# Four edits to a gated two-layer block: weight remainders moved ahead of the units, a guard row as one fp32 product, two products on GpSimd, a norm on ScalarE

## The chip, the cores and the metric

The kernel runs on one core of a Trainium2 chip. The metric is the device time of one execution in microseconds (us). Names of engines: PE is TensorE, DVE is VectorE, ACT is ScalarE, POOL is GpSimd.

## The reference, cut to what matters

```python
x = x + tanh(g_xattn[0]) * wkv(w, u, layernorm(x), ctx)            # a decaying scan over 64 steps
x = x + tanh(g_ffn[0])   * ffn(layernorm(x), w_gate_up, w_proj)    # ternary weights, silu(gate)*up, rms norm, projection
x = x + tanh(g_xattn[1]) * attend(layernorm(x), ctx, mask)
x = x + tanh(g_ffn[1])   * linear(fp8(layernorm(x)), weight) + bias
# ternary_quant, on groups of 64 weights of a row:
#   scale = clip(mean(|w_g|), 1e-8);  q = clip(round(w_g / scale), -1, 1);  w_hat = q * scale
```

x has 16 x 64 tokens of 256 channels, w_gate_up is 2048 x 256 and w_proj 256 x 1024.

## The kernel before

The 1024 tokens lie in eight tiles of 128 and two halves of four tiles (h = 0 and 1). Every engine has its program written out by hand, and semaphores join them.

**Front.** For each half, PE turns the normed x to channel-major in banks 0 and 1 (`front_keys`, L712) and adds a guard, the product of a row that depends on the decay with the row of time steps 0 to 63. The row is split into three bf16 parts that DVE makes (L1382 to L1392) and that one bf16 product of 65 rows adds (L715). ACT exponentiates the result (`front_keys`, L511), and DVE multiplies it with the context (`wkv_product`, L1137), scans and divides it. Between these, PE transposes six blocks of 1024 weight columns (`weight_transposes`, L737) and ACT takes them to SBUF as `wT` (L529). PE keeps busy with six spare products (`keep_warm`, L971), sums absolute weights by group (`weight_sums`, L747) and brings half 0 back to token-major (`y_back`, L794).

**Remainders.** For each of the six blocks in QUANT_ORDER, `weight_rest(n)` makes scale minus absolute weight in a pair of PSUM banks: four products, two with a stationary operand of 24 rows (L765) and two of 128 (L767). ACT copies the pair to `wscale` (`rest_in(n)`, L535), and DVE quantizes the block in four instructions (`quant_here` and `quant_sign`, L1249, L1250, L1256, L1239). Only the pair 6, 7 is used, so that a remainder waits for the copy of the one before. Remainders 0 and 1 stand ahead of the first units, 2 just ahead of unit 0, 3 in unit 0, 4 in unit 1, 5 in unit 3.

**Units.** Sixteen units n of 128 tokens by 512 hidden columns. PE does `gate(n)` and `up(n)` (four products of 512 columns each, L845 and L846), turns unit n-1 back (`h_back`, L878), projects unit n-2 (L904) and subtracts the rounded part (`h_left`, L884). ACT does `silu(n)` (L576), then the square and the two parts of h of unit n-1 (L583, L587, L591). DVE multiplies gate and up to `hbuf` (`ffn_mul(n)`, L1284) and fits all other work between these. `linear_weight` (PE L945 and ACT L596) prepares the last layer's weight in unit 4. Half 1 of the first layer lies within units 3 to 6: DVE does both products (L1137), two scans, two residuals with statistics (`mix_pair`, `ln_stats`) and two norms (`ln_apply(1, 4, 2, 2)` and `(1, 6, 2, 3)`, L1127), whose reciprocal deviation POOL makes (`power`, L414 and L415). PE turns these tiles with `ffn_in(2)` ahead of gate 8 and `ffn_in(3)` ahead of gate 10 (L810).

Of the kernel before, what the change touches and what calls it, by code (L numbers as in the profile page):

```python
# [36 lines left out]
def gated_blocks(nc, x, ctx_in, mask, g_xattn, g_ffn, w_decay, u_bonus, w_gate_up, w_proj,  # L37
# [24 lines left out]
    QUANT_ORDER = [0, 1, 4, 2, 3, 5]  # L62
    SCALE_ROWS = 24
# [4 lines left out]
    GUARD_ROWS = 65  # L68
# [4 lines left out]
    with ExitStack() as ctx:  # L73
# [31 lines left out]
        t_row = sb("t_row", [GUARD_ROWS, CT], BF16)  # L105
        ngrow = sb("ngrow", [1, C])
        ngres = sb("ngres", [1, C])
        ngres2 = sb("ngres2", [1, C], BF16)
        ngparts = sb("ngparts", [GUARD_ROWS, C], BF16)
# [260 lines left out]
        def _(pool):  # L370
            own = [0]

            def link(ins):
# [18 lines left out]
            pool.memset(group_spread[:, :, :], 0.0).then_inc(spread_0, 1)  # L392
            pool.wait_ge(spread_0, 1)
            spread = group_spread.rearrange("m k (s c) -> m k s c", s=2)
            pool.affine_select(out=spread, in_=spread, compare_op=ALU.not_equal, fill=1.0, base=0,
                               pattern=[[-2, BLOCKS], [-1, 2], [0, 64]], channel_multiplier=1).then_inc(spread_ready, 1)
# [20 lines left out]

            power(0, 0, TPC, 1)
            power(0, TPC, TPC, 2)
            power_and_shift(1, 0, TPC, 1)  # L420
# [28 lines left out]
            power(1, 4, 2, 2)  # L449
            power(1, 6, 2, 3)  # L450
# [29 lines left out]
        def _(act):  # L480
# [50 lines left out]
            def rest_in(n):  # L531

                p = QUANT_ORDER[n]
                act.wait_ge(rest_ps, n + 1)
                act.activation(wscale[:, p, :].rearrange("p (a b) -> p a b", a=2), ps[:, 6:8, :],  # L535
                               ACT.Copy).then_inc(rest_ready, 1)
# [82 lines left out]
            for n in range(UNITS):  # L619
# [38 lines left out]
            ln_apply(3, 0, 2, 2)  # L658
# [6 lines left out]
            ln_apply(3, 2, 2, 3)  # L665
# [25 lines left out]
        def _(pe):  # L691
# [10 lines left out]
            def front_keys(h):  # L702
                pe.wait_ge(xn_ready[0], h + 1)
                if h == 0:
                    pe.wait_ge(guard_rows, 6)
                    pe.wait_ge(const_ready, 1)
                for c in range(CH):
# [7 lines left out]
                    mm = pe.matmul(ps[:, c, :], ngparts[0:GUARD_ROWS, c * P:(c + 1) * P], t_row[0:GUARD_ROWS, :],  # L715
# [36 lines left out]
            def weight_rest(n):  # L752
# [17 lines left out]
            def spread_scales():  # L770

                pe.wait_ge(scale_max_ready, 1)
                t = pe.transpose(ps[:, 4, 0:16], scale_max[:, :].broadcast_to([16, P]), ident[0:16, 0:16])
# [24 lines left out]
            def ffn_in(k):  # L798
# [4 lines left out]
                if k == 0:  # L803
                    pe.wait_ge(xn_ready_act, 1)
                else:
                    pe.wait_ge(xn_ready[1], k)
# [15 lines left out]
            def channel_major(stage, q, ready):  # L822
# [6 lines left out]
                elif q < 2:  # L829
                    pe.wait_ge(xn_ready_act, q + 2)  # L830
# [18 lines left out]
            def gate(n):  # L849
                if n == 0:  # L850
                    pe.wait_ge(G_ready, CHUNKS * CH)
                    pe.wait_ge(xlo_ready, 2)
                    pe.wait_ge(wq_ready, WQ_GATE[0])
# [10 lines left out]
            def up(n):  # L864
                if n == 0:
                    pe.wait_ge(wq_ready, WQ_UP[0])
                if n == TPC:
# [19 lines left out]
            def project(n):  # L887
                i, f = unit(n)
                if n == 0:
                    pe.wait_ge(gmax_done, 1)  # L890
# [115 lines left out]
            weight_rest(0)  # L1006
            weight_rest(1)
            spread_scales()
            ffn_in(0)
# [3 lines left out]
            weight_rest(2)  # L1013
            for n in range(UNITS + 2):
# [83 lines left out]
        def _(dve):  # L1098
# [236 lines left out]
            def greatest(q):  # L1335
                first, n = PARTS[q]
                if q < 2:
                    dve.wait_ge(xn_ready_act, q + 2)
# [7 lines left out]
            dve.memset(ngparts[:, :], 0.0).then_inc(guard_rows, 1)  # L1346
# [11 lines left out]
            def power_of_two():  # L1358
                dve.wait_ge(gspread_ps, 1)
                dve.tensor_reduce(gmax_all[:, :], ps[:, 4, 0:16].rearrange("p (g n) -> p g n", g=2), AX_X,  # L1360
# [20 lines left out]
            dve.wait_ge(guard_rows, 2)  # L1381
            dve.tensor_copy(ngparts[0:1, :], ngrow[:, :]).then_inc(guard_rows, 1)  # L1382
# [3 lines left out]
            dve.wait_ge(guard_rows, 3)  # L1386
            dve.tensor_tensor(ngres[:, :], ngrow[:, :], ngparts[0:1, :], ALU.subtract).then_inc(guard_rows, 1)
            dve.wait_ge(guard_rows, 4)
            dve.tensor_copy(ngres2[0:1, :], ngres[:, :]).then_inc(guard_rows, 1)
            dve.tensor_copy(ngparts[32:33, :], ngres[:, :])  # L1390
            dve.wait_ge(guard_rows, 5)
            dve.tensor_tensor(ngparts[64:65, :], ngres[:, :], ngres2[:, :], ALU.subtract).then_inc(guard_rows, 1)  # L1392
# [26 lines left out]
            for n in range(UNITS):  # L1419
# [10 lines left out]
                if n == 3:  # L1430
                    wkv_product(2)
                    wkv_product(3)
# [12 lines left out]
                if n == 6:  # L1445
                    mix_pair(3)
                    ln_apply(1, 4, 2, 2)
# [130 lines left out]
```

## Time and profile before

| | |
|---|---|
| median of 3 runs | 144.17 us (143.52 to 144.33) |
| profiled execution | 144.26 us |
| its span in the trace | 142.5 us |
| PE, DVE, ACT, POOL busy | 84%, 83%, 59%, 26% of the span |
| mean granted clock of PE | 0.926 of full speed |

The span leaves out 1.76 us that lie around it. A time in the trace is counted from the span's start. A row of the timeline gives the start, the duration from start to end (the durations of queued instructions overlap, so pace is read from start to start), the engine, the line, output and inputs, and in brackets the engine's idle time ahead of it and who ended it.

### The profile page before, as it was taken

To read this page: it belongs to the slowest core of one execution; us is meant where nothing else is said; L and a number is where in the kernel's file an instruction comes from. 1 tells how busy PE (TensorE), PEld (TensorE's weight loads), DVE (VectorE), ACT (ScalarE), POOL (GpSimd) and SP (SyncE) were. 2 spreads that over 40 slices of the span, in tenths; PEclk is the share of its full clock that TensorE was granted. 3 is DMA by queue.
4 is the path that set the end of the run, shared out by engine and by line. 5 is a ranking of instruction groups with operands and counts; after the bars stand their busy time and mean duration, and the time that the engine had idled before them with its cause. 6 is when DMAs were issued, how large, how long until landed. Compare 5 with 4: busy or idle time off the path is not lost.

```text
span 142.5 us, 2199 instructions
## 1 busy us (share of the span) xinstructions
PE 119.5 (84%) x735; PEld 78.6 (55%) x735; DVE 118.3 (83%) x280; ACT 83.9 (59%) x158; POOL 37.0 (26%) x77
## 2 busy tenths in 40 slices
PE   5967799872999899999879999999967794993971
PEld 5856673312333365676436767767656572872660
DVE  5999999989957979999968979499977899948920
ACT  3397697037775686786557868747445345137131
POOL 7907000042000000000265320394355244010700
PEclk9999999965559999999999999999999999599599
DMA  4999940000000000000000000000000000000224
GB/s 136 285 364 350 386 85 2 0 0 0 0 0 0 0 5 2 0 0 0 0 0 7 0 0 5 0 0 0 2 5 0 0 0 2 0 0 0 70 81 147
DMA packets 7093, 6.89 MB, mean 48 GB/s; under 512 B 1320, under 2 KB 6826, under 8 KB 7082
## 3 DMA queue, kind: packets, MB, share of 16 engines
q1 hardware_dynamic: 7072, 6.75, 14.6%
q8 instruction: 6, 0.10, 0.3%
q14 instruction: 5, 0.04, 0.1%
q10 hardware_dynamic: 10, 0.00, 0.0%
HBM read 5.70 MB, written 1.05 MB: 47 GB/s over the span
## 4 chain that ended last, share of the span: by engine, by line
PE 44%; DVE 25%; ACT 11%; DMA 6%; issue 5%; SPq 5%; POOL 2%; DVEq 0%; ACTq 0%
PE ps L845 7%; PE ps L846 7%; DMA wgu_raw<-in_L_ffn_w_gate_up_dram 6%; PE ps L904 5%; DVE xs L1204 4%; PE ps L878 4%; DVE stats L1115 4%; PE ps L765 3%; PE ps L767 3%; PE ps L810 2%; DVE kv L1529 2%; ACT wscale L535 2%; ACT wT L529 2%; PE ps L1091 2%; PE ps L747 2%
## 5 line engine op out<-in xcount | busy, mean ns | idle before, releaser
L845 PE MATMUL ps<-wT,xhi 128*128 128x512 bf16 x64 | 25.2, 394 | 1.0 <-ACT xlo L546 1.0
L846 PE MATMUL ps<-wT,xlo 128*128 128x512 bf16 x64 | 25.0, 391 | 0.0
L414 POOL TENSOR_SCALAR ve<-mv 128x2 f32<-128x2 f32 (+2 forms) x12 | 2.8, 236 | 59.2 <-DVE mv L1121 59.1
L904 PE MATMUL ps<-wT,wgu_raw 128*128 128x256 bf16 x128 | 16.6, 273 | 0.1
L904 PEld LDWEIGHTS ps<-wT,wgu_raw 128*128 128x128 f16 x128 | 12.4, 98 | 1.6 <-DVE wgu_raw L1271 0.3
L1115 DVE BATCH_NORM_STATS2 stats<-xs 128x6 f32<-128x256 f32 x32 | 12.3, 415 | 1.1 <-DMA xs<-in_x_dram 0.7
L587 ACT ACTIVATE wgu_raw<-ps 128x512 f16<-128x512 f32 x16 | 9.5, 597 | 5.5 <-PE ps L878 5.0
L1127 DVE TENSOR_SCALAR xn<-xs,mv,rstd 128x256 f32<-128x256 f32 x26 | 9.5, 407 | 2.9 <-POOL rstd L415 2.1
L535 ACT ACTIVATE wscale<-ps 128x1024 bf16<-128x1024 f32 x6 | 6.1, 1023 | 9.2 <-PE ps L767 9.2
L1284 DVE SCALAR_TENSOR_TENSOR hbuf<-ps,pscale,sil 128x512 f32<-128x512 f32 x11 | 8.2, 748 | 3.2 <-PE ps L846 3.2
L845 PEld LDWEIGHTS ps<-wT,xhi 128*128 128x128 f16 x64 | 6.4, 101 | 7.7 <-ACT xlo L546 1.5
L878 PE MATMUL ps<-ident,hbuf 128*128 128x128 f32 x64 | 9.7, 275 | 1.0 <-DVE wgu_raw L1271 1.0
L846 PEld LDWEIGHTS ps<-wT,xlo 128*128 128x128 f16 x64 | 6.5, 101 | 7.3 <-issue 1.1
L583 ACT ACTIVATE wgu_raw<-hbuf 128x512 f32<-128x512 f32 x16 | 10.0, 626 | 0.6 <-DVE hbuf L1284 0.6
L1091 PE MATMUL ps<-wl_parts,wabs 128*128 128x256 bf16 x48 | 7.2, 322 | 3.3 <-DVE wabs L1535 3.3
L415 POOL TENSOR_TENSOR rstd<-ve,minus_half 128x2 f32<-128x2 f32 (+2 forms) x12 | 9.4, 787 | 1.0
L878 PEld LDWEIGHTS ps<-ident,hbuf 128*128 128x128 f32 x64 | 7.6, 140 | 3.0 <-DVE hbuf L1284 1.3
L576 ACT ACTIVATE sil<-ps 128x512 f32<-128x512 f32 x11 | 6.6, 596 | 3.3 <-PE ps L846 3.2
L1091 PEld LDWEIGHTS ps<-wl_parts,wabs 128*128 128x128 bf16 x48 | 5.4, 115 | 5.4 <-issue 2.7
L836 PE MATMUL ps<-ident,xn 128*128 128x128 f32 x32 | 5.4, 282 | 2.8 <-DVE xn L1127 2.8
L1271 DVE TENSOR_TENSOR wgu_raw<-ps,wgu_raw 128x512 f16<-128x512 f32 x8 | 5.5, 684 | 2.7 <-ACT wgu_raw L587 2.7
L591 ACT ACTIVATE wgu_raw<-ps 128x512 f16<-128x512 f32 x8 | 4.8, 597 | 4.8 <-PE ps L884 4.8
(172 smaller groups left out, 279.0 us busy)
## 6 DMA issues: line engine op xcount, KB each, us to landing
wgu_raw<-in_L_ffn_w_gate_up_dram SPq DMA_DIRECT2D x4, 512.0 KB, 8.9
ctx_sb<-in_ctx_dram SPq DMA_DIRECT2D x2, 512.0 KB, 7.4
wp_raw<-in_L_ffn_w_proj_dram SPq DMA_DIRECT2D x1, 1024.0 KB, 10.2
out_dram<-xs SPq DMA_DIRECT2D x4, 256.0 KB, 2.1
xs<-in_x_dram SPq DMA_DIRECT2D x2, 256.0 KB, 2.9
xs<-in_x_dram SPq DMA_DIRECT2D x1, 512.0 KB, 7.0
wlin_raw<-in_L_ffn_weight_dram SPq DMA_DIRECT2D x1, 256.0 KB, 9.1
bias_bc<-in_L_ffn_bias_dram SPq DMA_DIRECT2D x1, 128.0 KB, 8.6
```

Of the source, the lines that this page charges most:

```text
L415: pool.tensor_tensor(rstd[:, stage, tiles], ve[:, stage, tiles], minus_half[:, 0:n], ALU.pow).then_inc(rstd_ready[stage], 1)
L535: act.activation(wscale[:, p, :].rearrange("p (a b) -> p a b", a=2), ps[:, 6:8, :], ACT.Copy).then_inc(rest_ready, 1)
L583: act.activation(sq[:, n % 2, :], hbuf[:, n % 2, :], ACT.Square, accum_out=ssq[:, f, i:i + 1]).then_inc(sq_ready, 1)
L587: act.activation(hhi[:, n % 2, :], ps[:, 3, :], ACT.Copy).then_inc(hhi_ready, 1)
L845: pe.matmul(ps[:, bank, :], xhi[:, h, c, o:o + P], w, start=(c == 0), stop=False)
L846: mm = pe.matmul(ps[:, bank, :], xlo[:, h, c, o:o + P], w, start=False, stop=(c == CH - 1))
L878: t = pe.matmul(ps[:, 3, j * P:(j + 1) * P], hbuf[:, n % 2, j * P:(j + 1) * P], ident[:, :], start=(j == 0), stop=False, is_transpose=True ...
L904: mm = pe.matmul(proj_at(i), part[:, n % 2, j * P:(j + 1) * P], wT[:, GU_PAIRS + f, j * C:(j + 1) * C], start=(first and f == 0 and j == 0 ...
L1091: mm = pe.matmul(ps[:, LAST_BANK[k], i * C:(i + 1) * C], xq[:, c, n * P:(n + 1) * P], wl_parts[:, part, c, :], start=False, stop=(c == CH ...
L1115: now = step(dve.bn_stats(stats[:, i, :], res[:, i, :]))
L1127: ins = dve.tensor_scalar(xn[:, i, :], res[:, i, :], mv[:, stage, i, 0:1], rstd[:, stage, i:i + 1], ALU.subtract, ALU.mult)
L1284: dve.scalar_tensor_tensor(out=hbuf[:, b, :], in0=ps[:, 1 + b, :], scalar=(pscale if n < TANH_FROM else pscale_half)[:, 0:1], in1=sil[:, b ...
```

## The change

1. **Remainders.** All six `weight_rest` stand ahead of unit 0, four before and two behind `spread_scales`, alternating between bank pairs 6, 7 and 4, 5. ACT has `rest_in` 0 to 3 ahead of its norm of tiles 0 and 1, 4 behind it, and 5 behind `silu(0)`. `invert(2)` moves behind the first `xn_low` pair. `spread_scales` uses bank 1. `gate(0)` waits for the first xn part alone, `up(0)` also for the scales' maximum. `linear_weight` moves to unit 0 on PE and unit 1 on ACT; on PE it waits for all six copies, as before.
2. **Guard row.** One fp32 product of one row by 512 columns replaces the bf16 product of 65 rows. DVE's zero fill and five instructions that made the parts go. POOL's two instructions on `group_spread` move behind its first power.
3. **Half 1's products** go from DVE (unit 3) to POOL, ahead of its power for half 0's second norm, with a wait for DVE's first scan of half 1.
4. **Half 1's norm** goes from DVE (units 6 and 7) to ACT (units 6 and 8). POOL makes a shift as well as the deviation for it.

```diff
-            power(1, 4, 2, 2)
-            power(1, 6, 2, 3)
+            power_and_shift(1, 4, 2, 2)
+            power_and_shift(1, 6, 2, 3)
...
             power(0, TPC, TPC, 2)
+            pool.wait_ge(den_scanned, 1)
+            wkv_product(2)
+            wkv_product(3)
             power_and_shift(1, 0, TPC, 1)
...
-            rest_in(0)
-            rest_in(1)
-            invert(2)
+            for n in range(4):
+                rest_in(n)
             ln_apply(1, 0, TPC // 2, 1)
+            rest_in(4)
             xn_high(0)
             xn_high(1)
             xn_low(0)
             xn_low(1)
+            invert(2)
             invert(3)
...
+                    if n == 6:
+                        ln_apply(1, 4, 2, 2)
+                    if n == 8:
+                        ln_apply(1, 6, 2, 3)
                 if n == 0:
-                    rest_in(2)
-                    rest_in(3)
+                    rest_in(5)
                 if n == 1:
-                    rest_in(4)
-                if n == 3:
-                    rest_in(5)
-                if n == 4:
                     linear_weight()
...
-                    mm = pe.matmul(ps[:, c, :], ngparts[0:GUARD_ROWS, c * P:(c + 1) * P], t_row[0:GUARD_ROWS, :],
+                    mm = pe.matmul(ps[:, c, :], ngrow[0:1, c * P:(c + 1) * P], t_row[0:1, :],
                                    start=False, stop=True, skip_group_check=True)
...
-                else:
-                    pe.wait_ge(rest_ready, n)
+                if n >= 2:
+                    pe.wait_ge(rest_ready, n - 1)
...
-                    bank = 6 + a
+                    bank = REST_BANK[n % 2] + a
...
-            weight_rest(0)
-            weight_rest(1)
+            for n in range(4):
+                weight_rest(n)
             spread_scales()
+            weight_rest(4)
+            weight_rest(5)
             ffn_in(0)
             ffn_in(1)
             ffn_in_left(0)
             ffn_in_left(1)
-            weight_rest(2)
...
                 if n == 0:
-                    weight_rest(3)
-                if n == 1:
-                    weight_rest(4)
-                if n == 3:
-                    weight_rest(5)
-                if n == 4:
                     linear_weight()
```

PE's order, with its waits, from `up(0)` to `gate(1)`, before:

```order
L845 MATMUL ps<-wT,xhi 128x512 [waits wq_ready]
L846 MATMUL ps<-wT,xlo 128x512
L845 MATMUL ps<-wT,xhi 128x512
L846 MATMUL ps<-wT,xlo 128x512
L765 MATMUL ps<-scales,group_spread 128x512 [waits wabs_ready,wsc_ready,rest_ready]
L767 MATMUL ps<-wabs,neg_bf 128x512
L765 MATMUL ps<-scales,group_spread 128x512
L767 MATMUL ps<-wabs,neg_bf 128x512
L845 MATMUL ps<-wT,xhi 128x512 [waits sil_ready]
```

And of the change, from the same `up(0)`:

```order
L853 MATMUL ps<-wT,xhi 128x512 [waits gmax_done,wq_ready]
L854 MATMUL ps<-wT,xlo 128x512
L853 MATMUL ps<-wT,xhi 128x512
L854 MATMUL ps<-wT,xlo 128x512
L956 MATMUL ps<-ident,wlin_raw 128x128 [waits rest_ready,in_wlin]
```

The remainder of unit 0 has gone, and `linear_weight` (L956), which waits for all six copies by ACT, stands there in its place, ahead of `gate(1)`.

ACT's order from the first norm of half 0 (`xn`, here of the second norm stage) to `silu(1)`, before:

```order
L516 ACTIVATE ratio<-ratio 128x512
L518 ACTIVATE ratio<-ratio 128x512
L523 ACTIVATE xn<-xs,shift,rstd 128x256 x2
L541 ACTIVATE xhi<-ps 128x2x256 x2
L546 ACTIVATE xlo<-ps 128x2x256 x2
L516 ACTIVATE ratio<-ratio 128x512
L518 ACTIVATE ratio<-ratio 128x512
L569 ACT_TABLE_LOAD
L576 ACTIVATE sil<-ps 128x512
L535 ACTIVATE wscale<-ps 128x1024 x2
L576 ACTIVATE sil<-ps 128x512
```

And of the change (`ratio` is `invert`, `wscale` is `rest_in`):

```order
L530 ACTIVATE xn<-xs,shift,rstd 128x256 x2
L543 ACTIVATE wscale<-ps 128x1024
L549 ACTIVATE xhi<-ps 128x2x256 x2
L554 ACTIVATE xlo<-ps 128x2x256 x2
L523 ACTIVATE ratio<-ratio 128x512
L525 ACTIVATE ratio<-ratio 128x512
L523 ACTIVATE ratio<-ratio 128x512
L525 ACTIVATE ratio<-ratio 128x512
L578 ACT_TABLE_LOAD
L585 ACTIVATE sil<-ps 128x512
L543 ACTIVATE wscale<-ps 128x1024
L585 ACTIVATE sil<-ps 128x512
```

A copy has come in ahead of `xhi`, both inversions now stand together just ahead of the table load and `silu(0)`, and one copy instead of two stands between the first two silu.

## Rows read from the trace of the kernel before

**Rows 1.** The page: granted PE clock, in 40 slices of 3.56 us.

```profile
PEclk9999999965559999999999999999999999599599
```

**Rows 2.** Windows of 1 us: busy of each engine, then the granted clock (PEclk).

```profile
29.00:30.00 1.00, 0.74 (x2) 0.20 (x2) 1.00 (x6) 0.20 (x1) 0.00 (x0) 0.65 0.00 0
...
42.00:43.00 1.00, 1.00 (x4) 0.30 (x2) 0.00 (x0) 1.00 (x2) 0.00 (x0) 0.53 0.00 0
```

**Rows 3.** Timeline of DVE and of POOL in the front.

```profile
7.94 1.38 DVE L1127 TENSOR_SCALAR xn<-xs,mv,rstd 128x256 f32<-128x256 f32 x4
...
6.30 1.04 POOL L415 TENSOR_TENSOR rstd<-ve,minus_half 128x4 f32<-128x4 f32 x1
```

**Rows 4.** Timeline of PE: half 1's keys, the last transposes, sums.

```profile
18.75 0.38 PE L715 MATMUL ps<-t_row,ngparts 65*128 65x512 bf16 x1
19.39 1.97 PE L737 MATMUL ps<-ident,wp_raw 128*128 128x128 f32 x16 [0.26 <-DMA wp_raw<-in_L_ffn_w_proj_dram]
21.20 1.46 PE L971 MATMUL ps<-wabs,neg_bf 128*128 128x512 bf16 x6
22.91 2.76 PE L747 MATMUL ps<-wabs,group_sum 128*24 128x512 bf16 x12 [0.26 <-ACT wT L529]
```

**Rows 5.** The fp32 products of L960, called eight times: records, and two calls.

```profile
L960 PE MATMUL ps<-bias_g,ident x16: 379/379/635, 109.7 to 127.4; 128*128 128x256 f32 x16
...
109.66 1.03 PE L960 MATMUL ps<-bias_g,ident 128*128 128x256 f32 x4
110.53 1.03 PE L963 MATMUL ps<-xs,ident 128*128 128x256 f32 x4
```

**Rows 6.** Timeline of PE: first product of remainder 1, later work.

```profile
29.26 0.60 PE L765 MATMUL ps<-scales,group_spread 24*128 24x512 bf16 x1 [1.12 <-ACT wscale L535]
...
37.47 0.61 PE L819 MATMUL ps<-xhi,neg_ident 128*128 128x512 f16 x1 [0.24 <-ACT xhi L541]
```

**Rows 7.** Timeline of ACT ahead of the units and in unit 0.

```profile
33.62 1.08 ACT L523 ACTIVATE xn<-xs,shift,rstd 128x256 f32<-128x256 f32 x2
...
38.61 0.62 ACT L516 ACTIVATE ratio<-ratio 128x512 f32<-128x512 f32 x1
...
39.91 1.28 ACT L569 ACT_TABLE_LOAD   x1
41.97 0.60 ACT L576 ACTIVATE sil<-ps 128x512 f32<-128x512 f32 x1 [0.78 <-PE ps L846]
42.47 1.02 ACT L535 ACTIVATE wscale<-ps 128x1024 bf16<-128x1024 f32 x1
```

**Rows 8.** Timeline of DVE: `hbuf` of units 0, 1, 2 and 6, two products.

```profile
43.47 0.75 DVE L1284 SCALAR_TENSOR_TENSOR hbuf<-ps,pscale,sil 128x512 f32<-128x512 f32 x1 [2.13 <-PE ps L846]
...
46.85 0.75 DVE L1284 SCALAR_TENSOR_TENSOR hbuf<-ps,pscale,sil 128x512 f32<-128x512 f32 x1
...
51.23 0.75 DVE L1284 SCALAR_TENSOR_TENSOR hbuf<-ps,pscale,sil 128x512 f32<-128x512 f32 x1 [0.92 <-PE ps L846]
...
55.27 1.28 DVE L1137 TENSOR_TENSOR kv<-kv,ctxT 128x512 f32<-128x512 f32 x2
...
67.95 0.75 DVE L1284 SCALAR_TENSOR_TENSOR hbuf<-ps,pscale,sil 128x512 f32<-128x512 f32 x1
```

**Rows 9.** Timeline of POOL: two-input fp32 instructions of 512 columns.

```profile
93.81 1.25 POOL L431 TENSOR_TENSOR wp_raw<-wl,wl_parts 128x512 f32<-128x512 f32 x1
...
132.25 1.67 POOL L474 TENSOR_TENSOR kv<-kv,wsign 128x512 f32<-128x512 f32 x1 [6.99 <-DVE wsign L1525]
```

**Rows 10.** Timeline: `ffn_in(2)` and gate 8 on PE; a deviation with shift on POOL.

```profile
70.40 0.63 PE L810 MATMUL ps<-ident,xn 128*128 128x128 f32 x4 [0.42 <-DVE xn L1127]
...
73.77 0.39 PE L845 MATMUL ps<-wT,xhi 128*128 128x512 bf16 x1 [0.96 <-ACT xlo L546]
...
99.06 0.19 POOL L402 TENSOR_SCALAR ve<-mv 128x2 f32<-128x2 f32 x1 [2.05 <-DVE mv L1121]
...
100.39 0.19 POOL L407 TENSOR_TENSOR shift<-nmean,rstd 128x2 f32<-128x2 f32 x1
```

More of the change, by code:

```diff
@@ L62, in gated_blocks @@
     QUANT_ORDER = [0, 1, 4, 2, 3, 5]
+    REST_BANK = [6, 4]
     SCALE_ROWS = 24
@@ L416, in power, with wkv_product @@
                                    ALU.pow).then_inc(rstd_ready[stage], 1)
-            power(0, 0, TPC, 1)
+            def wkv_product(k):
+                v = ctxT[:, k % CH, CT:NTOK].rearrange("p (b t) -> p b t", t=T)
+                pool.wait_ge(ctxT_ready, k + 1)
+                pool.wait_ge(G_ready, k + 1)
+                pool.tensor_tensor(kv[:, k, 1, :, 1:T + 1], kv[:, k, 0, :, 1:T + 1], v, ALU.mult).then_inc(GV_ready, 1)
+            power(0, 0, TPC, 1)
+            pool.memset(group_spread[:, :, :], 0.0).then_inc(spread_0, 1)
+            pool.wait_ge(spread_0, 1)
+            spread = group_spread.rearrange("m k (s c) -> m k s c", s=2)
+            pool.affine_select(out=spread, in_=spread, compare_op=ALU.not_equal, fill=1.0, base=0,
+                               pattern=[[-2, BLOCKS], [-1, 2], [0, 64]], channel_multiplier=1).then_inc(spread_ready, 1)
             power(0, TPC, TPC, 2)
+            pool.wait_ge(den_scanned, 1)
+            wkv_product(2)
+            wkv_product(3)
             power_and_shift(1, 0, TPC, 1)
@@ L533, in rest_in @@
                 p = QUANT_ORDER[n]
+                bank = REST_BANK[n % 2]
                 act.wait_ge(rest_ps, n + 1)
-                act.activation(wscale[:, p, :].rearrange("p (a b) -> p a b", a=2), ps[:, 6:8, :],
+                act.activation(wscale[:, p, :].rearrange("p (a b) -> p a b", a=2), ps[:, bank:bank + 2, :],
                                ACT.Copy).then_inc(rest_ready, 1)
@@ L657, in _ @@
             channels_in(qT, 2, qT_ps, qT_ready)
-            ln_apply(3, 0, 2, 2)
+            ln_apply(3, 0, 2, 4)
             channels_in(qT, 3, qT_ps, qT_ready)
@@ L664, in _ @@
             attn_in(3)
-            ln_apply(3, 2, 2, 3)
+            ln_apply(3, 2, 2, 5)
             softmax_exp(4)
@@ L704, in front_keys @@
                 if h == 0:
-                    pe.wait_ge(guard_rows, 6)
+                    pe.wait_ge(guard_rows, 1)
                     pe.wait_ge(const_ready, 1)
@@ L772, in spread_scales @@
                 pe.wait_ge(scale_max_ready, 1)
-                t = pe.transpose(ps[:, 4, 0:16], scale_max[:, :].broadcast_to([16, P]), ident[0:16, 0:16])
+                t = pe.transpose(ps[:, 1, 0:16], scale_max[:, :].broadcast_to([16, P]), ident[0:16, 0:16])
                 t.then_inc(gspread_ps, 1)
@@ L802, in ffn_in @@
                 pe.wait_ge(res_ready[1], (1, 1, 2, 3)[k])
-                if k == 0:
-                    pe.wait_ge(xn_ready_act, 1)
+                if k == 1:
+                    pe.wait_ge(xn_ready[1], 1)
                 else:
-                    pe.wait_ge(xn_ready[1], k)
+                    pe.wait_ge(xn_ready_act, (1, 0, 2, 3)[k])
                 for c in range(CH):
@@ L829, in channel_major @@
                 elif q < 2:
-                    pe.wait_ge(xn_ready_act, q + 2)
+                    pe.wait_ge(xn_ready_act, q + 4)
                 else:
@@ L851, in gate @@
                     pe.wait_ge(G_ready, CHUNKS * CH)
+                    pe.wait_ge(xlo_ready, 1)
+                    pe.wait_ge(wq_ready, WQ_GATE[0])
+                if n == 2:
                     pe.wait_ge(xlo_ready, 2)
-                    pe.wait_ge(wq_ready, WQ_GATE[0])
                 if n == TPC:
@@ L866, in up @@
                     pe.wait_ge(wq_ready, WQ_UP[0])
+                    pe.wait_ge(gmax_done, 1)
                 if n == TPC:
@@ L889, in project @@
                 if n == 0:
-                    pe.wait_ge(gmax_done, 1)
+                    pe.wait_ge(rest_ready, PAIRS)
                     pe.wait_ge(wT_ready, PAIRS)
@@ L1337, in greatest @@
                 if q < 2:
-                    dve.wait_ge(xn_ready_act, q + 2)
+                    dve.wait_ge(xn_ready_act, q + 4)
                 else:
@@ L1451, in _ @@
                 if n == 7:
-                    ln_apply(1, 6, 2, 3)
                     ffn_out(0)
```

26 lines of the change are left out of this document (2 added, 24 removed).

## The prediction, made before the changed kernel ran

> **What bounds the kernel now.** I read the page first, for the clock. PE is granted full speed but for four slices from about 28 to 43 us and two dips near the end of about a slice each, 3.56 us [rows 1]. The windows place the fall: 0.65 in the microsecond from 29 means full speed (2.4 GHz) up to 29.3 and half (1.2 GHz) from there, and 0.53 in that from 42 puts the rise at 42.94 [rows 2]. Ahead of the fall PE had paused for 1.12 us, because remainder 1 needs the bank pair that ACT was still copying [rows 6]. Ahead of the rise it had worked without a pause since 37.47, for 5.5 us [rows 6]. Then I read the timelines of the three engines. From unit 0 on DVE waits in few places: 2.13 us ahead of `hbuf` 0, 0.92 ahead of `hbuf` 2 [rows 8]. From there until `hbuf` 6 it is full but for 0.16 us, so an instruction taken from it there is worth its pace; work taken from PE is worth something only where DVE waits for PE. Ahead of the units ACT and DVE share the path: `silu(0)` at 41.97 waited 0.78 us for PE [rows 7].
>
> **Guard row.** Before, half 1's guards cost 0.22 us each from start to start (512 columns at 2.4 GHz are 0.213). The trace has no fp32 product of one row. L960 is called eight times and has 16 records, so a call is two records, and two calls of 256 columns take 0.87 us (109.66 to 110.53) [rows 5]: 1.7 ns a column, 0.86 us for 512. Were a call one record, it would be 0.43; that bound, against 0.86, stays for the range. I take 0.86, because the count of calls is plain: +0.64 each, +1.28 for a half. In half 0 DVE's parts are gone: its norm, at 7.94 before, can start when POOL's power ends. That power ended at 7.34 [rows 3] and now starts about 0.6 earlier, so the norm starts near 6.75 and what PE loses it has won beforehand; the transfers that follow hide the rest. In half 1 nothing is won. PE's last keys would end at 20.25 instead of 18.97, of which the wait for `wp_raw` until 19.39 covers 0.42 [rows 4]. Transposes and spare products follow (3.1 us, 19.39 to 22.52), then the sums: 23.4 instead of 22.91 [rows 4]. That is **+0.47 us** on all that follows, since `y_back` stands behind the sums and DVE's residual waits for it.
>
> **Remainders.** At full clock one is about 1.27 us from start to start (four products of 512 columns, 0.86, and what their weight loads add), and ACT's copy 1.02 [rows 7]; with two pairs PE never waits for ACT. Six go from 27.28 to 35.0, without the pause that came ahead of the fall, so I take the clock to stay full here. ACT then does copy 3 (to 33.4), its norm of two tiles (0.93), copy 4 (0.92), four xn parts (until 37.7, set by PE's transposes from 35.0), two inversions of 1.30 each (38.61 to 39.91 for one) and the table load of 1.28 [rows 7]: 37.7 + 2.6 + 1.28 = 41.6 for `silu(0)`, 0.4 earlier than before. Copy 5 ends at 43.1, and **`linear_weight` on PE waits for it**, with `gate(1)` queued behind. Before, only remainder 3 stood there.
>
> DVE's quantization of blocks 0 and 1 starts 0.47 late, so `gate(0)` is at 38.05 and `up(0)` at 40.8. PE now pauses from about 37.0 to 38.05, from 38.9 to 40.8 and until 43.2: more than the pause after which the clock fell [rows 6]. So I take half clock from about 40 until PE has worked through for 3.6 us (it was that short in the dips [rows 1]) to 5.5 us (as above). From 43.2 that is 46.8 to 48.7. Then `up(0)` ends at 42.5 and `hbuf` 0 is at 42.65 (43.47 before). `linear_weight` costs 0.85, `gate(1)` and `up(1)` 1.71 each: `hbuf` 1 at 47.6, **0.75 us later** than 46.85 [rows 8], DVE waiting 1.6 us. `hbuf` 2 needs DVE's quantization (3.4 us from `hbuf` 1) and PE's turn of unit 0, its copy, and gate and up 2 (3.5 us from the end of `up(1)`): both give 51.05, against 51.23, 0.2 early. From here the clock is full. PE has 3.25 us of work a unit and lost 1.2 us in units 1 and 3; DVE has 3.4, and sets the pace.
>
> *TensorE: Matmul & The Clock Gate* of the Trainium skill, in its closing table, "Why this matters for your kernels", holds that throughput drops come from pauses longer than any of these; by it the clock would stay full and the sum would be that of the second case below.
>
> **Products.** DVE loses two instructions in unit 3, 0.6 us each from start to start (both 1.28 from start to end): -1.2 us, as it had no wait there [rows 8]. POOL has them from 26.5. An instruction of this form takes 1.25 or 1.67 us [rows 9], so they end by 29.0 or 29.9, and POOL's next power is due at 30.7. Hidden either way; if they did run into it, `silu(0)` would be late by the excess. With 0.2 from above, 1.2 here and the 0.16 that DVE waited, `hbuf` 6 is at 66.4 against 67.95 [rows 8], **1.55 early**.
>
> **Norm.** DVE loses two norms of 0.65 and a wait of 0.42. But the way from statistics to gate 8 gets longer: POOL's deviation with shift takes 1.52 us (99.06 to 100.58) [rows 10] where 1.0 did, ACT takes 1.08 [rows 7] where DVE took 0.75, and `silu(7)` is queued behind that norm on ACT, so square and `xhi` come after it. `ffn_in(2)` would start at 69.15 against 70.40, and gate 8, 3.37 us behind it before [rows 10], is now 3.75 behind it: 72.9 against 73.77. So 1.55 becomes 0.87. In units 8 and 9 the second norm does the same in small, 0.1 more: **0.8 early** at gate 10. Behind it nothing changes in order, PE, ACT and DVE hand over to each other, and I carry 0.8 us to the end.
>
> **Sum.** 144.26 - 0.8 = 143.46; the profiled execution lies 0.09 above the median of 144.17, so I say **143.4 us**.
>
> **How it could go otherwise.**
> 1. *As summed*, half clock until 46.8 to 48.1: 142.4 to 143.8. A rise at 46.8 saves 0.5, an fp32 call at 0.43 saves the 0.47; the two give the lower end, the errors of a schedule put together by hand the upper. Chance 0.5.
> 2. *The clock stays full through the pauses.* Then `hbuf` 1 is at 45.5 and `hbuf` 2 at 48.85, 2.2 earlier than in the sum: 141.2. For it: PE pauses near 1 us elsewhere (0.96 ahead of gate 8 [rows 10]) without a fall. Against it: here pauses make up two thirds of 6 us. Chance 0.12.
> 3. *Half clock beyond unit 1.* In unit 1 PE waits some 0.65 us for ACT's copy of the turned unit, from 48.1. If the clock has not risen by then, the unbroken work starts anew and it rises near 52: `hbuf` 2 at 52.2 to 53.0 instead of 51.05. The sum loses 1.15 to 1.95: 144.5 to 145.3. Chance 0.2.
> 4. *Slower for one reason: the run of remainders loses the clock itself.* Half of its products have a 24-row operand [rows 6]. If those count for little, the fall comes near 29.3 as before and remainders 2 to 5 take 2.15 us each: PE is done at 38.5, its transposes take twice as long, `silu(0)` is at 45.8 and `hbuf` 1 at 49.7, 2.1 after the sum's: 145.5, and up to 147 where the clock stays low in the units. It decides if the clock is at half for more than two remainders. Against it: the sums, 24 columns wide, passed at full clock [rows 4]. Chance 0.08.
> 5. *It doesn't reach the end:* the time saved waits in the tail (a dip of the clock that falls elsewhere): 143.9 to 144.4. Chance 0.1.
>
> A measurement of this kernel tells about 0.5%, 0.72 us, from no change: faster is below 143.45, slower above 144.89. Faster holds 0.33 of case 1, case 2 and 0.02 of the rest: 0.47. Within it: 0.17 of case 1, 0.08 of case 3 and 0.09 of case 5: 0.34. Slower: 0.12 of case 3 and 0.07 of case 4: 0.19. The range takes cases 1 and 5, the nearer part of 3 and the edge of case 2: 141.4 to 145.0. Alone, case 1 is 142.4 to 143.8.
>
> **What the profile after would show.** Guards of two records, 0.86 us from start to start, and sums at 23.4; six remainders in 7.7 us at clock 1.00; `silu(0)` near 41.6 and PE's `linear_weight` near 43.2, its wait ended by ACT's copy; a clock of 0.5 there; `hbuf` 1 near 47.6 with a wait for PE ahead of it, 2 near 51.0, 6 near 66.4; gate 8 near 72.9. The prediction is wrong if the clock falls during the remainders or not at all, or if PE instead of DVE sets the pace of units 2 to 6.

## The result, and the profile after

The changed kernel takes **148.87 us** (median of 4 runs, 146.66 to 151.11) against 143.84 (4 runs, 143.28 to 144.33). The ratio is **1.0256, 95% interval 1.0181 to 1.0332**: 2.6% slower, where 143.4 was forecast. Ratios are made without runs that lie over 1.5% above the fastest of their kernel, medians with them, so that in a kernel whose runs scatter the ratio can be nearer to 1 than the medians are.

The profiled execution took 149.0 us (span 147.2). The page after, granted PE clock in 40 slices of 3.68 us:

```profile
PEclk9997589999998579999999999999999999599699
```

The clock is now low in slices 4 to 6 too, about 13 to 19 us, where [rows 1] shows 9. All that follows on the clock of this kernel is read from this one execution; the mean granted clock of the four is 0.930, 0.929, 0.974 (146.66 us) and 1.000 (148.73 us); the last of these is taken up again under what is left open. Windows of PE (busy, granted clock, DMA share, GB/s) place both falls:

```profile
12.00:13.00 1.00, 1.00 (x5) 0.84 1.10 348
13.00:14.00 1.00, 1.00 (x2) 0.50 1.10 347
...
19.00:20.00 1.00, 1.00 (x9) 0.75 0.12 18
46.00:47.00 1.00, 0.63 (x3) 0.91 0.00 0
...
53.00:54.00 1.00, 0.40 (x2) 0.68 0.00 0
```

Half clock runs from 12.7 to 19.5 and from 46.8 to 53.6. The second is the fall that the prediction expected ahead of unit 1; the first it did not have. The timeline of PE from there to the sums, which answers to [rows 4]:

```profile
10.68 0.66 PE L720 MATMUL ps<-ident,xn 128*128 128x128 f32 x4 [2.27 <-DVE xn L1133]
11.27 1.12 PE L723 MATMUL ps<-t_row,ngrow 1*128 1x512 f32 x2
12.32 0.81 PE L720 MATMUL ps<-ident,xn 128*128 128x128 f32 x4
13.06 2.07 PE L723 MATMUL ps<-t_row,ngrow 1*128 1x512 f32 x2
15.07 3.67 PE L745 MATMUL ps<-ident,wgu_raw 128*128 128x128 f32 x16
...
22.16 1.12 PE L723 MATMUL ps<-t_row,ngrow 1*128 1x512 f32 x2
23.22 0.66 PE L720 MATMUL ps<-ident,xn 128*128 128x128 f32 x4
...
28.05 2.76 PE L755 MATMUL ps<-wabs,group_sum 128*24 128x512 bf16 x12
```

PE waits 2.27 us for DVE's norm, its transposes run at half clock, a guard call is 1.06 us from start to start (22.16 to 23.22), and the sums are at 28.05 instead of 22.91: **5.14 late**. Why the norm is late stands in the timelines of DVE and of POOL, which answer to [rows 3]:

```profile
6.82 3.81 DVE L1133 TENSOR_SCALAR xn<-xs,mv,rstd 128x256 f32<-128x256 f32 x4 [0.52 <-POOL rstd L407]
```

```profile
6.67 1.37 POOL L418 MEMSET group_spread<- 24x1536 bf16 x1
8.18 1.66 POOL L421 TENSOR_SCALAR_AFFINE_SELECT group_spread<-group_spread 24x1536 bf16<-24x1536 bf16 x1 [0.15 <-POOL group_spread L418]
```

It starts at 6.82, as forecast (6.75), but takes 3.81 us instead of 1.38, and it ends 0.8 us after the two POOL instructions that the change moved beside it. DVE in the units, after [rows 8]: `hbuf` 1 at 52.66 waits 2.17 us for PE, and `hbuf` 6 is at

```profile
71.58 0.75 DVE L1290 SCALAR_TENSOR_TENSOR hbuf<-ps,pscale,sil 128x512 f32<-128x512 f32 x1
```

3.63 late. So the later edits won back 1.5 of the 5.14 by unit 6. Gate 10 is 4.45 late (85.61 against 81.16).

### The profile page after: what moved, and what is told of

Same layout as the page of the kernel before. It is cut to its first block, busy times and chain, and to the rows that moved or that the text cites. A ratio compares the mean times of both kernels' runs of the same rounds, so it can differ in the third digit from the quotient of the medians.

```text
span 147.2 us, 2198 instructions
## 1 busy us (share of the span) xinstructions
PE 123.4 (84%) x730; PEld 81.6 (55%) x739; DVE 116.6 (79%) x268; ACT 85.4 (58%) x162; POOL 38.7 (26%) x83
## 3 DMA queue, kind: packets, MB, share of 16 engines
q1 hardware_dynamic: 7072, 6.75, 14.0%
## 4 chain that ended last, share of the span: by engine, by line
PE 44%; DVE 31%; ACT 10%; issue 6%; POOL 4%; DMA 2%; DVEq 0%; ACTq 0%; POOLq 0%
PE ps L853 6%; PE ps L854 6%; PE ps L915 5%; DVE stats L1121 5%; PE ps L745 4%; PE ps L889 4%; DVE xn L1133 4%; DVE xs L1210 4%; PE ps L723 4%; PE ps L773 3%; PE ps L775 2%; DVE kv L1521 2%; PE ps L1097 2%; DMA xs<-in_x_dram 2%; POOL rstd L407 2%
## 5 line engine op out<-in xcount | busy, mean ns | idle before, releaser
L853 PE MATMUL ps<-wT,xhi 128*128 128x512 bf16 x60 | 23.8, 396 | 3.6 <-DVE gmax_all L1365 1.8
L854 PE MATMUL ps<-wT,xlo 128*128 128x512 bf16 x62 | 24.5, 395 | 0.2
L1133 DVE TENSOR_SCALAR xn<-xs,mv,rstd 128x256 f32<-128x256 f32 x22 | 10.5, 517 | 2.8 <-POOL rstd L407 2.2
L394 POOL TENSOR_SCALAR ve<-mv 128x2 f32<-128x2 f32 (+1 forms) x5 | 1.4, 273 | 40.5 <-DVE mv L1127 40.5
L889 PE MATMUL ps<-ident,hbuf 128*128 128x128 f32 x64 | 10.2, 284 | 1.1 <-DVE wgu_raw L1277 1.1
L406 POOL TENSOR_SCALAR ve<-mv 128x2 f32<-128x2 f32 (+2 forms) x10 | 1.9, 192 | 24.0 <-DVE mv L1127 24.0
```

Of the source, the lines that this page charges most:

```text
L853: pe.matmul(ps[:, bank, :], xhi[:, h, c, o:o + P], w, start=(c == 0), stop=False)
L854: mm = pe.matmul(ps[:, bank, :], xlo[:, h, c, o:o + P], w, start=False, stop=(c == CH - 1))
L889: t = pe.matmul(ps[:, 3, j * P:(j + 1) * P], hbuf[:, n % 2, j * P:(j + 1) * P], ident[:, :], start=(j == 0), stop=False, is_transpose=True ...
L1133: ins = dve.tensor_scalar(xn[:, i, :], res[:, i, :], mv[:, stage, i, 0:1], rstd[:, stage, i:i + 1], ALU.subtract, ALU.mult)
```

## The experiments

The first theory: the whole loss is in the front, in two parts. POOL's work beside DVE holds the norm up (A), and the guard's fp32 product of one row brings the clock down (C). Rivals: either alone does it; or the later edits lose as well. Four kernels divided the front.

**group_spread back in front, fp32 guard kept.**

```diff
+            pool.memset(group_spread[:, :, :], 0.0).then_inc(spread_0, 1)
...
             power(0, 0, TPC, 1)
-            pool.memset(group_spread[:, :, :], 0.0).then_inc(spread_0, 1)
...
             power(0, TPC, TPC, 2)
```

> The changed kernel with one thing undone: the two GpSimd instructions on group_spread stand ahead of its first power again, as before. Theory A (VectorE's first norm and GpSimd's group_spread instructions, which now run side by side, hold each other up: four norms take 3.81 us instead of 1.38, and TensorE, kept waiting for 2.3 us, loses its clock): the four norms take 1.4 us again, they end near 8.8, the clock does not fall ahead of 28 us, the weight sums start at 23.4 to 24.0 instead of 28.05, and the time is 4 to 5 us under the changed kernel, 143.2 to 144.5. Theory B (the fp32 guard product costs it, in the front by itself): the norms may be short, but the sums stay later than 26 us and the time is above 146.

Measured: median 147.1 us (10 runs, 143.98 to 148.78), ratio 1.0038 (0.997 to 1.0106). The ratio rests on the three runs of 143.98 to 145.88 us; the other seven, the profiled one among them, took 146.49 and more. In the profiled one the norm takes 1.38 us again, and yet the clock falls at 11.3 and the sums are at 26.28. So by its trace A alone does not explain the loss; by its ratio 0.4% of the 2.6% would be left without it, and not clear of none. What C costs has to be read from the kernel with the guard alone, below.

**group_spread moved, in the kernel before.** Nothing else of the change.

```diff
-            pool.memset(group_spread[:, :, :], 0.0).then_inc(spread_0, 1)
...
             power(0, 0, TPC, 1)
+            pool.memset(group_spread[:, :, :], 0.0).then_inc(spread_0, 1)
...
```

> The kernel before with one thing of the change: group_spread's two GpSimd instructions behind the first power. Theory A: the first norm (7.94 before) now stands beside them (7.4 to 10.4) and takes 3 us or more instead of 1.38; TensorE's keys start after 10.5 and the time is 1 to 5 us above before, more if the clock falls in the front. Theory B: within 0.5% of before, since group_spread is not needed until 26.8 us.

Measured: 146.33 us (4 runs), ratio 1.0102 (1.0033 to 1.017). PE waits 2.35 us for the norm, the clock is at half from 11.3 to 18.1, the sums are at 25.86: A costs 1.0% by itself (2 us on the medians). Here the norm takes its 1.38 us, but it starts at 10.29 instead of 7.94: two of the guard's parts ahead of it are held up, from 0.28 and 0.42 us to 1.57 and 1.92:

```profile
6.75 1.57 DVE L1390 CAST ngparts<-ngres 1x256 bf16<-1x256 f32 x1
8.34 1.92 DVE L1392 TENSOR_TENSOR ngparts<-ngres 1x256 bf16<-1x256 f32 x1
10.29 1.38 DVE L1127 TENSOR_SCALAR xn<-xs,mv,rstd 128x256 f32<-128x256 f32 x4
```

POOL's timeline of this kernel shows its memset from 6.81 to 8.18 and its select from 8.32 to 9.98. Each of the two DVE instructions ends within 0.3 us of the POOL instruction beside it.

**group_spread behind the second power, fp32 guard kept.** 

```diff
-            pool.memset(group_spread[:, :, :], 0.0).then_inc(spread_0, 1)
...
             power(0, TPC, TPC, 2)
+            pool.memset(group_spread[:, :, :], 0.0).then_inc(spread_0, 1)
...
```

> The changed kernel with group_spread's two instructions behind GpSimd's second power (near 13 us), beside VectorE's scans. Theory A: the norm starts at 6.8 and takes 1.4 us, TensorE's first keys stand at 8.3, sums near 23.4, time 142.7 to 144: the sum of my prediction, as its front term assumed. If the scans, with two inputs in memory, are held up by them in turn, 0.5 to 1 us of that is given back. Theory B: above 146.

Measured: 148.33 us (4 runs, 146.13 to 151.04), ratio 1.0141 (1.0027 to 1.0254). The norm takes 1.38 us and PE has no pause at 7 to 13 us, but in the profiled execution the clock falls at 13.3 and again at 23.6, and the sums are at 27.86. Waiting less for DVE did not save the clock.

**fp32 guard alone, in the kernel before.** DVE's zero fill and its five instructions go too, as in the change.

```diff
-                    mm = pe.matmul(ps[:, c, :], ngparts[0:GUARD_ROWS, c * P:(c + 1) * P], t_row[0:GUARD_ROWS, :],
+                    mm = pe.matmul(ps[:, c, :], ngrow[0:1, c * P:(c + 1) * P], t_row[0:1, :],
```

> The kernel before with the guard row as one fp32 product, all else as before. Theory A: the norm starts near 7.4 and takes 1.4 us; two products of 0.86 to 1.06 us more in each half make the sums start at 23.4 to 23.9 instead of 22.91: +0.5 to +1.0 us in all. Theory B (the guard is the cost): +4 us or more.

Measured: 146.55 us (10 runs), ratio 1.0112 (1.0068 to 1.0155). Its windows of PE:

```profile
12.00:13.00 1.00, 1.00 (x6) 1.00 1.09 347
13.00:14.00 1.00, 1.00 (x7) 0.98 1.10 352
14.00:15.00 1.00, 1.00 (x7) 0.50 1.15 369
```

PE is busy throughout here and in every microsecond from 5, and still the clock falls at 13.96, 3.2 us after the first guard product (10.73), and stays at half until 17.4. The sums are at 25.92. Each part costs by itself 1.0% and 1.1% (+2.05 and +2.27 us on the median of 144.28), and no pause is needed for the fall.

One thing differs here that no edit made. The same ten transposes, in the kernel before and in this one:

```profile
5.93 1.32 PE L986 MATMUL ps<-ident 128*128 128x128 f32 x10
```

```profile
5.96 2.40 PE L982 MATMUL ps<-ident 128*128 128x128 f32 x10
```

PE began this execution at half pace and kept it until shortly after 10 us, though the windows show 1.00 there; so its keys start at 9.85, where after a quick start, with nothing holding up the norm, they start at 8.9 to 9.4. It is a matter of the execution: the ten take 2.40 us in seven of the seventeen profiled ones and 1.31 in ten. Up to half a microsecond of the 3.01 at the sums may belong to it (with an fp32 product of 65 rows, tried below in two kernels, the sums are at 23.69 after a quick start and at 24.13 after a slow one). It does not decide the fall: the clock falls ahead of 20 us in the profiles of all four kernels with a one-row fp32 guard, in two of quick and two of slow starts, in both others with the moved `group_spread`, and in none of the remaining eleven, four of which start slowly. Is it the fp32, or the one row? Two kernels cross the two with the two there were.

**fp32 guard of 65 rows** in the kernel before. Rows 1 to 64 of `ngrow` are zero, and `t_row` has 65 rows too.

```diff
-        ngrow = sb("ngrow", [1, C])
+        ngrow = sb("ngrow", [65, C])
...
+                    mm = pe.matmul(ps[:, c, :], ngrow[0:65, c * P:(c + 1) * P], t_row[0:65, :],
```

> The kernel before with the guard as an fp32 product of 65 rows, of which 64 are zero, instead of one row (the product is the same). Theory: the one-row product is what brings the clock down some 3 us after it begins. Then here, with as many rows as the bf16 product had, the clock stays full through the front, the guards take the same 1.05 us each from start to start, the sums come at 23.5 to 24.5 and the time is 144.0 to 145.0 us. Rival: it is the fp32 product itself (its two passes and 2 us for a pair), whatever its rows: the clock falls at 13 to 14 us as with one row, sums near 25.9, 146.5 us.

Measured: 144.73 us (10 runs), ratio 1.005 (1.0003 to 1.0098). Page and timeline:

```profile
PEclk9999999985569999999999999999999999999969
```

```profile
18.39 1.02 PE L711 MATMUL ps<-t_row,ngrow 65*128 65x512 f32 x2
19.25 0.60 PE L708 MATMUL ps<-ident,xn 128*128 128x128 f32 x4
...
23.69 2.76 PE L743 MATMUL ps<-wabs,group_sum 128*24 128x512 bf16 x12
```

The clock stays full until 31.5, a guard is 0.86 us from start to start (18.39 to 19.25), to the hundredth what the prediction took, and the sums are at 23.69 (23.4 forecast).

**bf16 guard of one row**, in the kernel before. It leaves two of the guard's three parts out.

```diff
-                    mm = pe.matmul(ps[:, c, :], ngparts[0:GUARD_ROWS, c * P:(c + 1) * P], t_row[0:GUARD_ROWS, :],
+                    mm = pe.matmul(ps[:, c, :], ngparts[0:1, c * P:(c + 1) * P], t_row[0:1, :],
```

> The kernel before with its bf16 guard product cut to the first of its 65 rows, which leaves the two lower parts of the guard out. DVE makes them all the same, so only the rows of the product differ. If few rows alone bring the clock down, it falls in the front here too, near 12 to 14 us, and the sums come 1 to 3 us late: 145 to 147 us. If not (a bf16 product of 512 columns is 0.22 us and soon over), nothing moves: sums at 22.9, 144.2 us, ratio 0.997 to 1.003.

Measured: 144.46 us (10 runs), ratio 0.9999 (0.9953 to 1.0046), clock row of the page as [rows 1] but for one of the two late dips. Here a guard is 0.32 us from start to start (17.93 to 18.25) instead of 0.22, but nothing hangs on that. So of the four guards, each in one profiled execution or more, only the fp32 product of one row brings the clock down.

**The change without both front edits.** Bf16 parts and `group_spread` as before the change; edits 1, 3 and 4 stay. Against the changed kernel:

```diff
-                    mm = pe.matmul(ps[:, c, :], ngrow[0:1, c * P:(c + 1) * P], t_row[0:1, :],
+                    mm = pe.matmul(ps[:, c, :], ngparts[0:GUARD_ROWS, c * P:(c + 1) * P], t_row[0:GUARD_ROWS, :],
...
+            pool.memset(group_spread[:, :, :], 0.0).then_inc(spread_0, 1)
...
             power(0, 0, TPC, 1)
```

> The change without both of its edits in the front: the guard row keeps its three bf16 parts and its product of 65 rows, and POOL makes group_spread ahead of its first power. Left are the remainders ahead of the units with linear_weight in unit 0, half 1's products on POOL and half 1's norm on ACT. If the loss is the front's alone, the sums stay at 22.9 and the clock stays full until the units; from the sums to hbuf 6 the change won 1.5 us and lost 0.6 to 0.8 of it until gate 10, so hbuf 6 is at 66.4, gate 10 at 80.3 and the time about 143.3 us, ratio 0.990 to 0.997. Rival: the later edits lose too (the clock in units 1 to 3 and the longer way to gate 8 cost what the remainders give): 144.0 to 145.0, ratio 1.000 to 1.006.

Measured: 144.58 us (12 runs, 142.62 to 148.08) against 144.46, ratio 0.9987 (0.9929 to 1.0045): the loss is gone, but no gain is left either. DVE gains until near the end. `hbuf` 6 is at 65.49 (67.95 before, 2.46 early), the last `hbuf` at 101.70 (1.62 early), and DVE's last instruction at 134.06 (1.67 early). What follows it, on PE, before and in this kernel:

```profile
136.48 2.79 PE L1091 MATMUL ps<-wl_parts,wabs 128*128 128x256 bf16 x24 [1.05 <-DVE wabs L1535]
```

```profile
134.81 4.41 PE L1101 MATMUL ps<-wl_parts,wabs 128*128 128x256 bf16 x24 [2.24 <-DVE wabs L1541]
```

```profile
134.00:135.00 1.00, 0.19 (x2) 0.87 0.78 262
135.00:136.00 1.00, 1.00 (x6) 0.50 0.00 0
```

The last 24 products start 1.67 earlier and take 1.62 longer, since the dip of the clock now lies on them (half from 134.7); before, it lay on the 24 ahead of them (4.45 us from 130.98). The fastest of the 12 runs, 142.62 us, has a mean clock of 0.988 where the profiled one has 0.973.

**The change without the fp32 guard.** Of the diff above the product alone, with DVE's parts; `group_spread` stays behind the first power.

> The change with the guard row in three bf16 parts as before, but with group_spread behind POOL's first power. If DVE's slow first norm beside group_spread is enough to make PE lose its clock in the front, PE pauses some 2 us ahead of the keys, the clock is at half from 12 to 18 us, the sums come at 25.5 to 26.5 and the time is 146 to 147 us. If only the one-row fp32 product takes the clock, the pause alone costs its length where PE has slack, the sums are at 23 to 24 and the time is 143.5 to 144.5 us.

Measured: 146.25 us (4 runs, 145.03 to 151.32), ratio 1.0108 (1.0007 to 1.0209). The clock is at half from 13.1 to 16.5, after a pause of 2.17 us, and the sums are at 24.95, earlier than expected. It dips on the last 24 products too.

**The whole change with both causes taken out**: `group_spread` in front, 65 rows of fp32 in the diffs as above.

> The whole change, but with group_spread ahead of POOL's first power and with the fp32 guard product over 65 rows, of which 64 are zero (the product is the same). Theory: the change's loss is all in the front, from the clock that the one-row fp32 product brings down and from group_spread beside DVE's norm. Then the clock stays full until unit 1, the guards take 0.86 us each from start to start, the sums come at 23.2 to 23.9, and the time is that of the later edits alone plus 0.3: 144.6 to 145.2 us. Rival: in the changed kernel something else in the front holds PE up too; then the sums are past 25 and the time is 146 to 147.5 us.

Measured: 145.06 us (10 runs), ratio 1.0026 (0.9981 to 1.0072); after a slow start the clock is full from 10.4 to 41.1 us, the sums are at 24.13 and `hbuf` 6 at 66.91. So 64 rows of zeros and five lines in their old place take the change's 2.6% down to 0.3%, within the interval of no difference.

**Spare products in the tail**, on the kernel without front edits.

```diff
+                if k == 0:
+                    pe.wait_ge(amax_done, 1)
+                if k in (0, 2):
+                    keep_warm(8, 7, wT)
                 pe.wait_ge(xq_ready[k == 3], 1 if k == 3 else k + 1)
```

> The change without both front edits, with eight spare bf16 products of 512 columns on PE (into bank 7, which nothing reads any more) ahead of the waits for the first and the third part of the last layer. Without them the 1.6 us won until DVE's last instruction (134.06 against 135.73) were lost again because the clock's dip fell on the last 24 products, 134.9 to 138. If the dip is what keeps the gain from the end, and PE's pauses of 2.2 us ahead of it bring it on, the clock stays full there: 142.4 to 143.2 us, ratio 0.985 to 0.995. Rival: the dip comes anyway, or the gain was not lost to it: 144.2 to 144.8 us as without them.

Measured: 142.52 us (6 runs, 142.09 to 143.45), ratio 0.989 (0.9842 to 0.9938). The last products run at full clock:

```profile
132.29 1.89 PE L986 MATMUL ps<-wT,neg_bf 128*128 128x512 bf16 x7
134.69 2.79 PE L1105 MATMUL ps<-wl_parts,wabs 128*128 128x256 bf16 x24 [0.51 <-DVE wabs L1545]
```

**The same spare products in the kernel before.**

> The kernel before with the same spare products ahead of the first and third part of the last layer. Its own dips stand at 119 to 124 and at 131.8 to 135, where less hangs on PE. If the spare products only keep a dip off the last 24 products, they are worth little here: 143.6 to 144.2 us, ratio 0.993 to 0.999. If they are worth as much as in the changed kernel (2 us), then the gain of the version with them there was theirs and not that of the later edits: 142.2 to 142.8 us.

Measured: 144.05 us (12 runs), ratio 0.999 (0.9954 to 1.0026). There they are worth nothing that can be measured, and edits 1, 3 and 4 without them nothing either (ratio 0.9987). Only together do they give the 1.1%: the edits bring it to DVE's last instruction, and the tail lets it through.

**linear_weight back in unit 4**, on the kernel without front edits.

```diff
-                if n == 0:
+                if n == 4:
                     linear_weight()
```

> The change without both front edits and with linear_weight in unit 4 on PE and ACT, as before the change. In unit 0 PE no longer waits for the copy of remainder 5. If that wait and the half clock behind it are what make hbuf 1 late (46.84), hbuf 1 is at 45.2 to 45.5, the pace of DVE, the clock keeps full there, hbuf 6 is at 64.0 to 64.6 instead of 65.49, and the time is 0 to 1.5 us less than without this (where the dip in the tail falls decides how much arrives): 143.0 to 144.6 us. Rival: the pauses ahead of gate 0 and up 0 bring the clock down anyway and linear_weight costs its 0.87 us in unit 4: hbuf 6 at 65.3 to 66, 144.6 us.

Measured: 142.8 us (6 runs, 140.89 to 143.89), ratio 0.9811 (0.9745 to 0.9877). From `hbuf` 0 to `hbuf` 1 are 3.42 us (42.56 to 45.98) without a wait, where it was 4.96 (41.88 to 46.84). `hbuf` 6 is at 64.94. In this profiled execution the dip lay on the last products again (4.46 us).

**Half 1's norm back on DVE**, on the kernel without front edits (edit 4 undone).

```diff
-            power_and_shift(1, 4, 2, 2)
-            power_and_shift(1, 6, 2, 3)
+            power(1, 4, 2, 2)
+            power(1, 6, 2, 3)
...
-                    if n == 6:
-                        ln_apply(1, 4, 2, 2)
...
                     mix_pair(3)
+                    ln_apply(1, 4, 2, 2)
```

> The change without both front edits and with half 1's norm on DVE as before. On ACT it stood in for 1.3 us of DVE's work but lengthened the way from the statistics to gate 8, and silu queued behind it: hbuf was 2.46 us early in unit 6, 1.98 in unit 8 and 1.64 in unit 10. If that is the norm's doing, hbuf 8 is here at 73.3 to 73.6 (73.93 with the norm on ACT), hbuf 10 at 80.7 to 81.0 (81.55), and what reaches DVE's last instruction is 2.2 to 2.5 us instead of 1.67; the time, with the dip in the tail, 143.8 to 144.6 us. Rival: DVE's 1.3 us come back in full: hbuf 8 at 74.5 or later, 144.8 to 145.5 us.

Measured: 143.03 us (12 runs), ratio 0.9911 (0.9873 to 0.9949). From `hbuf` 6 to the last are 35.37 us (65.18 to 100.55), as in the kernel before (67.95 to 103.32), where with the norm on ACT they are 36.21 (65.49 to 101.70): the norm on ACT cost 0.84. DVE's last instruction is at 132.89.

**Half 1's products back on DVE**, on the kernel with the spare products.

```diff
-            pool.wait_ge(den_scanned, 1)
-            wkv_product(2)
-            wkv_product(3)
...
                 if n == 3:
+                    wkv_product(2)
+                    wkv_product(3)
                     num_scan(2)
```

> The change without both front edits, with the spare products in the tail, and with half 1's two products on DVE in unit 3 as before. The prediction put them at 1.2 us. If DVE sets the pace of unit 3, hbuf 4 is 1.2 us later against hbuf 3 than the 3.33 that it is with them on POOL, and hbuf 6 is at 66.4 to 66.8; the time is 143.5 to 143.9 us. Rival: PE's pace of 3.25 us a unit hides part: 0.5 to 0.8 us, 143.0 to 143.3.

Measured: ratio 0.9944 (0.9896 to 0.9992) against 0.989 (0.9842 to 0.9938) with the products on POOL, intervals that overlap; the 12 runs scatter from 142.31 to 148.39 us (median 144.32). From `hbuf` 3 to `hbuf` 4 are 4.53 us (57.66 to 62.19) where with the products on POOL it is 3.32 to 3.33 in the profiles: 1.20 us, as forecast. Its profiled execution showed something else, in the windows of PE:

```profile
30.00:31.00 1.00, 1.00 (x4) 0.76 0.00 0
31.00:32.00 1.00, 1.00 (x3) 0.50 0.00 0
...
40.00:42.00 2.00, 1.76 (x8) 0.81 0.00 0
```

The clock fell within the six remainders and rose 10 us later; `silu(0)` was so late that `hbuf` 0 waited 4.48 us for it.

**What paid, together**: remainders ahead of the units and products on POOL from the change, everything else as before it, spare products in the tail. On the kernel without front edits this is the sum of three diffs above: `linear_weight` in unit 4, the norm on DVE, `keep_warm` ahead of the last products.

> What was best together: the remainders ahead of the units and half 1's products on POOL as in the change; the guard row, group_spread, linear_weight (unit 4) and half 1's norm (DVE) as before the change; spare products in the tail. Moving linear_weight back gave 0.5 us at hbuf 6 to 10 in the profiles, the norm on DVE 0.7 to 1.1 more at hbuf 10, and the spare products 1 to 2 us at the end. If they add: DVE's last instruction at 132.3 to 132.9, 141.0 to 141.8 us, ratio 0.975 to 0.984. Rival: the gains share one wait and only the largest counts: 142.3 to 142.8 us.

Measured: **140.55 us** (7 runs, 139.93 to 143.71) against 144.28, ratio **0.9749 (0.9698 to 0.98)**, 2.5% faster than the kernel before, and below the 141.0 to 141.8 us that were expected. The run of 143.71 is the profiled one, and in it the clock fell within the remainders, at 29.7.

## Why the prediction was wrong, point by point

**Guard row: the step that failed.** The prediction summed the front to +0.47 us at the sums; it was +5.14. Two things in it did not hold. First, it priced the five DVE instructions that go and the fp32 calls that come, and gave the two POOL instructions that the same edit moves no price at all: they are 1.37 and 1.65 us long, and stand where DVE's norm is due. Beside them the norm took 3.81 us for 1.38. The page *SBUF — State Buffer* of the Trainium skill, section "Who interferes with whom", says that a GpSimd instruction and a DVE cast or tensor_scalar in a two-port mode exclude each other for a whole instruction. The traces agree (a cast of 0.28 us took 1.57 beside the memset), and the rule spoke against this edit before it ran. Second, it took the clock for safe in the front: "what PE loses it has won beforehand" and "the transfers that follow hide the rest" count the length of the guard calls alone. With one row it is not safe, with 65 it is. Alone, the parts cost 1.0% (moved `group_spread`, 2.05 us on the medians) and 1.1% (one-row fp32, 2.27 us), at the sums 2.95 and 3.01 us. Together they are 5.14 us at the sums; the whole change takes 2.6%, 5.0 us on the medians. How much of each is waiting and how much is the half clock was not separated.

**The size of a guard call** was right at 0.86 for 65 rows, and wrong for the one row that the change uses: 1.06. Both have two records a call, as argued from L960. Even with 65 rows, where the call had the size that the forecast used, the sums were 0.78 late and not 0.47.

**Remainders.** Six of them ran at clock 1.00 in the profile after and in the version without front edits, 1.28 us each (1.27 forecast). With the sums at 23.18 there, `silu(0)` is at 41.18 (41.6 from 23.4 forecast). PE's `linear_weight` waits for ACT's copy of remainder 5 at 42.84 (43.2), `hbuf` 1 is at 46.84 (47.6) and `hbuf` 6 at 65.49 (66.4). The fall came at 42.6 and the rise at 46.0, nearer together than assumed (40 to 46.8 or later), which with the 0.2 us of the sums is where the 0.9 us come from. The second case, a clock that stays full through the pauses, and the rule that the prediction names beside it, did not hold: in the profile after the clock fell at 46.8, after pauses of 0.72 and 1.78 us. Moving `linear_weight` back took 1.54 us off that unit, but only 0.55 reach `hbuf` 6. In that execution `hbuf` 0 was 0.68 later (the clock fell at 39.5 there), and another 0.31 went between units 1 and 6, some of it in unit 4, where `linear_weight` costs PE time again.

**Products** were worth 1.20 us, as forecast, and POOL had them done from 31.54 to 33.86 in the profile after, with nobody waiting for them.

**Norm.** The forecast was a loss of 0.75 between `hbuf` 6 and gate 10. It was 0.82 by `hbuf` (2.46 early in unit 6, 1.64 in unit 10), and undoing it gave 0.84 back: the mechanism and nearly the size.

**The end.** "Carry 0.8 us to the end" failed in another way. 1.67 us reached DVE's last instruction, and the dip on the last 24 products took 1.62 of them. That was case 5, given a chance of 0.1; spare products in the tail show its mechanism by removing it. **Case 4**, the clock lost within the remainders, did not happen in the profile after, nor in eight others with all six remainders ahead of the units, but in two. What decides from run to run whether it happens was not found out. So the later edits brought DVE what they should, the tail kept it from the time (144.58 us without the front edits, 143.4 forecast), and the slower time came from the front alone.

**Left open.** Why a one-row fp32 product brings the clock down and one of 65 rows does not, is not shown; only that it is neither the type nor the row count alone. No row count between 1 and 65 was tried. Nor is the changed kernel's own time fully accounted for by the clock: one of its four runs took 148.73 us with a mean granted clock of 1.000. No trace of that run is kept, so whether its clock records are incomplete, or something else costs as much there, stays open.

## What to carry to other kernels

Of a moved instruction ask not only whether its own result is early enough, but what the other engines do beside it: 3 us of POOL work put next to DVE cost 1.0% of the whole, 2 us on the medians. A gain shown at an early mark is not yet one at the end; follow it through DVE's and PE's last rows, and keep PE at work ahead of the last products if the clock dips there. When a change bundles several edits, undo them one by one: here two of them were worth 2.5% together with a few spare products, and two others cost more than that.

## What the runs showed of the hardware that was not expected

- A matmul with a single row is slower from start to start than one of 65 rows with the same 512 columns: fp32 1.06 us against 0.86, bf16 0.32 against 0.22.
- The granted clock fell to half while PE was busy without a pause from 5 us on (fp32 guard alone; up to about 10 us at half pace), 3.2 us after the first one-row fp32 product, and came back after 3.4 us. With zero rows added it did not fall there.
- The windows show a granted clock of 1.00 also where PE still runs at half pace at the start: sixteen transposes take 3.67 us from 1.52 in the kernel before, and 1.97 from 19.39 [rows 4].
- Also POOL is held up: its select of 1.65 us took 2.60 beside DVE's scans, when it was put behind the second power.
